# An LSTM with a low-rank adapter: VectorE transposes the pre-activations in PSUM instead of the hidden state in SBUF

## The reference

```python
def step(carry, xz_t):                      # LSTM: 16 sequences, 256 steps, 256 units
    prev_h, prev_c = carry
    z = xz_t + prev_h @ Wh                  # xz = x @ Wx + b, [16, 1024]
    ai, af, ao, ag = jnp.split(z, 4, axis=1)
    next_c = sigmoid(af) * prev_c + sigmoid(ai) * tanh(ag)
    next_h = sigmoid(ao) * jnp.tanh(next_c)
    return (next_h, next_c), next_h
x = x + lstm(x, cond)                       # [16, 256, 256]
# adapter: low-rank factors a1, b1, a2, b2 are made from cond by a small network
mid = gelu(x @ base_down + (x . a2) . b2)
out = mid @ base_up.T + (b1 . mid) . a1
x = x + out
```

## Time and profile before

| | us |
|---|---|
| median of 3 runs | 647.21 (644.83 to 648.85) |
| profiled execution, its time | 645.61 |
| profiled execution, its span | 643.6 |
| TensorE busy / VectorE / ScalarE | 604.5 / 430.3 / 412.8 |

### The profile page before, as it was taken

How to read it: one execution, slowest core, us unless ns; L and a number is a source line. 1 busy time by engine, 2 the same in 40 slices (tenths; PEclk the granted TensorE clock), 3 DMA queues, 4 the chain that set the end, 5 groups by cost and what they waited for, 6 DMA issues and landing times.

```text
span 643.6 us, 34068 instructions
## 1 busy us (share of the span) xinstructions
PE 604.5 (94%) x14176; PEld 450.4 (70%) x14176; DVE 430.3 (67%) x2292; ACT 412.8 (64%) x2414; POOL 38.2 (6%) x78
## 2 busy tenths in 40 slices
PE   8789999999998999999999999999999999999997
PEld 5555556777776677777777777777777777777876
DVE  3566556777776677677777777777777676777663
ACT  2465565666666666666666666666666666666672
POOL 3000000000000000000000000000000000000000
PEclk9799999999999999999999999999999999999999
DMA  4883522022223112322211222322123223212201
GB/s 160 223 210 130 175 43 42 22 29 52 53 52 53 28 33 48 53 52 53 52 33 29 47 53 52 53 52 38 26 45 52 53 52 53 39 35 25 54 20 34
DMA packets 31467, 38.71 MB, mean 60 GB/s; under 512 B 3601, under 2 KB 29505, under 8 KB 30290
## 3 DMA queue, kind: packets, MB, share of 16 engines
q1 hardware_dynamic: 31282, 36.51, 26.9%
q0 software_dynamic: 32, 0.03, 0.0%
HBM read 15.55 MB, written 4.19 MB: 31 GB/s over the span
## 4 chain that ended last, share of the span: by engine, by line
PE 63%; DVE 25%; ACT 6%; issue 4%; DMA 1%; SPq 0%; ACTq 0%; DVEq 0%
PE z L666 31%; PE x_bank L488 9%; DVE gates L815 8%; DVE prod L810 8%; PE aux L514 8%; ACT gates L405 6%; DVE h_t L825 5%; PE z_o L666 4%; PE out_bank L595 4%; DVE hid L820 3%; PE aux L499 2%; PE out_bank L545 1%; PE out_bank L537 1%; DMA seed<-proj 1%; PE x_bank L514 1%
## 5 line engine op out<-in xcount | busy, mean ns | idle before, releaser
L666 PE MATMUL z<-wh,h_t 128*16 128x96 f32 x8160 | 226.6, 249 | 26.7 <-DVE h_t L825 16.3
L666 PEld LDWEIGHTS z<-wh,h_t 128*16 128x16 f32 x8160 | 154.0, 96 | 132.3 <-DVE h_t L825 110.4
L810 DVE SCALAR_TENSOR_TENSOR prod<-gates 128x64 f32<-128x64 f32 x512 | 113.2, 221 | 155.5 <-ACT gates L405 140.7
L405 ACT ACTIVATE gates<-z 128x96 f32<-128x96 f32 x512 | 106.2, 250 | 149.9 <-PE z L666 149.5
L488 PE MATMUL x_bank<-wx,x_t 128*128 128x256 f32 x512 | 150.3, 398 | 0.5 <-ACT x_t L323 0.5
L415 ACT ACTIVATE tanc<-gates 128x32 f32<-128x32 f32 x512 | 114.5, 224 | 48.1 <-DVE gates L815 47.8
L329 ACT ACTIVATE z<-seed 128x96 f32<-128x96 f32 x512 | 125.1, 245 | 5.6 <-DMA seed<-proj 5.6
L825 DVE STREAM_TRANSPOSE h_t<-hid 128x32 f32<-128x32 f32 x512 | 108.4, 212 | 17.4
L815 DVE SCALAR_TENSOR_TENSOR gates<-prod 128x32 f32<-128x32 f32 x512 | 98.1, 192 | 17.5
L666 PE MATMUL z_o<-wh,h_t 128*16 128x64 f32 x4080 | 104.8, 219 | 1.6 <-issue 1.6
L820 DVE SCALAR_TENSOR_TENSOR hid<-gate_o,tanc 128x32 f32<-128x32 f32 x512 | 98.3, 192 | 1.2 <-ACT tanc L415 1.2
(11 more groups left out here) (106 smaller groups left out, 350.0 us busy)
## 6 DMA issues: line engine op xcount, KB each, us to landing
seed<-proj SPq DMA_DIRECT2D x128, 128.0 KB, 3.9
w<-in_L_cond_W SPq DMA_DIRECT2D x4, 2048.0 KB, 9.7
x_nat<-in_x SPq DMA_DIRECT2D x32, 128.0 KB, 3.8
out<-y_nat SPq DMA_DIRECT2D x32, 128.0 KB, 3.8
wx<-in_L_cond_Wx SPq DMA_DIRECT2D x2, 512.0 KB, 5.2
wh<-in_L_cond_Wh SPq DMA_DIRECT2D x2, 256.0 KB, 6.1
wh<-in_L_cond_Wh SPq DMA_DIRECT2D x1, 512.0 KB, 6.1
w<-in_L_cond_W SPq DMA_DIRECT2D x1, 256.0 KB, 4.3
```

Source lines behind the costliest of these rows:

```text
L405: act.activation(gates[s % 2][m][:, 0:GC], z_bank[m][:, 0:GC], ACT.Tanh, scale=0.25).then_inc(gates_ready[m], 1)
L666: ins = pe.matmul(dst, h_prev[:, kc, :], rhs, start=False, stop=(kc == 1), skip_group_check=True)
L810: dve.scalar_tensor_tensor(prod[m][:, :], now[:, 0:2 * C], 1.0, now[:, 2 * C:4 * C], ALU.add, ALU.mult).then_inc(prod_ready[m], 1)
```

## The change

VectorE transposes z within its PSUM bank as soon as it is complete: z_bank[m][:, 0:96] into columns 96 to 191 of the same bank (zt), and the 64 columns of o_bank into its columns 64 to 127 (zt_o). After that units are on partitions and the 16 batch rows are columns, so that the padding can be left out: the gates' tanh writes 48 columns instead of 96, the o gate's is one instruction of 32 columns instead of two, prod has 32 columns instead of 64, cell, tanc and hid have 16 instead of 32. The product that was hid goes straight into h_t, and the two transposes of hid are gone. tanc lies in PSUM: half 0 in a bank of its own, half 1 in o_bank behind zt_o. ScalarE's seed_o waits for h of half 1 (ht_ready[1]) besides, since it writes into the bank that holds tanc of half 1. The first of the new hidden products (new_hidden with m = 0) waits for the o gate and for tanc.

ScalarE's order is now: gates 0, gates 1, o gate, tanc 0, seed 0, tanc 1, seed 1, seed o. VectorE's is: turn 0, turn 1, prod 0, turn o, cell 0, prod 1, cell 1, hidden 0, hidden 1. TensorE's list is the same as before.

```diff
--- before.py
+++ after.py
@@ -108,11 +108,9 @@
 
         h_first = sb("h_first", [P, NM, B])
 
-        gates = [[sb(f"gates{i}_{m}", [P, GC + C]) for m in range(NM)] for i in range(2)]
-        gate_o = sb("gate_o", [P, OC])
-        prod = [sb(f"prod{m}", [P, 2 * C]) for m in range(NM)]
-        tanc = [sb(f"tanc{m}", [P, C]) for m in range(NM)]
-        hid = [sb(f"hid{m}", [P, C]) for m in range(NM)]
+        gates = [[sb(f"gates{i}_{m}", [P, 4 * B]) for m in range(NM)] for i in range(2)]
+        gate_o = sb("gate_o", [P, NM * B])
+        prod = [sb(f"prod{m}", [P, 2 * B]) for m in range(NM)]
         h_t = [sb(f"h_t{i}", [P, NM, TB, 32]) for i in range(2)]
 
         xp = [sb(f"xp{i}", [P, NM, P]) for i in range(2)]
@@ -129,6 +127,10 @@
         aux = psum("aux")
         out_bank = psum("out_bank")
         x_bank = [psum(f"x_bank{i}") for i in range(2)]
+        tanc_bank = psum("tanc")
+        tanc = [tanc_bank[:, 0:B], o_bank[:, 2 * OC:2 * OC + B]]
+        zt = [z_bank[m][:, GC:2 * GC] for m in range(NM)]
+        zt_o = o_bank[:, OC:2 * OC]
         mid_bank, up_bank = (aux, x_bank[0]), (out_bank, x_bank[1])
 
 
@@ -162,7 +164,8 @@
         prod_ready = [sem(f"prod_ready{m}") for m in both]
         cell_ready = [sem(f"cell_ready{m}") for m in both]
         tanc_ready = [sem(f"tanc_ready{m}") for m in both]
-        hid_ready = [sem(f"hid_ready{m}") for m in both]
+        turned = [sem(f"turned{m}") for m in both]
+        turned_o = sem("turned_o")
         ht_ready = [sem(f"ht_ready{m}") for m in both]
         xp_ready = sem("xp_ready")
         u_psum, u_ready = ([sem(f"{n}{i}") for i in lanes] for n in ("u_psum", "u_ready"))
@@ -401,26 +404,26 @@
                     ahead, s_next = (k, s + 1) if s < TB - 1 else (k.plus(1), 0)
 
                     def gates_of(m):
-                        act.wait_ge(z_ready[m], n)
-                        act.activation(gates[s % 2][m][:, 0:GC], z_bank[m][:, 0:GC], ACT.Tanh,
+                        act.wait_ge(turned[m], n)
+                        act.activation(gates[s % 2][m][:, 0:3 * B].rearrange("p (g b) -> p g b", b=B),
+                                       zt[m].rearrange("p (g c) -> p g c", c=C)[:, :, 0:B], ACT.Tanh,
                                        scale=0.25).then_inc(gates_ready[m], 1)
 
-                    def tanh_o(m):
-
-                        cols = slice(C * m, C * (m + 1))
-                        return act.activation(gate_o[:, cols], o_bank[:, cols], ACT.Tanh, scale=0.25)
+                    def tanh_o():
+                        act.wait_ge(turned_o, n)
+                        act.activation(gate_o[:, :].rearrange("p (m b) -> p m b", b=B),
+                                       zt_o.rearrange("p (m c) -> p m c", c=C)[:, :, 0:B], ACT.Tanh,
+                                       scale=0.25).then_inc(gate_o_ready, 1)
 
                     def tanh_cell(m):
                         act.wait_ge(cell_ready[m], n)
-                        act.activation(tanc[m][:, :], gates[(s + 1) % 2][m][:, GC:GC + C], ACT.Tanh,
+                        act.activation(tanc[m], gates[(s + 1) % 2][m][:, 3 * B:4 * B], ACT.Tanh,
                                        scale=0.5).then_inc(tanc_ready[m], 1)
 
                     gates_of(0)
                     gates_of(1)
-                    act.wait_ge(zo_ready, n)
-                    tanh_o(0)
+                    tanh_o()
                     tanh_cell(0)
-                    tanh_o(1).then_inc(gate_o_ready, 1)
                     if more:
                         act.wait_ge(gates_ready[0], n)
                         seed_bank(ahead.par, s_next, 0)
@@ -429,6 +432,7 @@
                         act.wait_ge(gates_ready[1], n)
                         seed_bank(ahead.par, s_next, 1)
                         act.wait_ge(gate_o_ready, n)
+                        act.wait_ge(ht_ready[1], n + 1)
                         seed_o(ahead.par, s_next)
 
                     if s == TB - 2 and (front or k.p == 0):
@@ -768,7 +772,7 @@
             dve.memset(zeros[:, :], 0.0).then_inc(zeroed, 1)
             dve.memset(hid_win[:, :, :], 0.0).then_inc(zeroed, 1)
             for m in both:
-                dve.memset(gates[0][m][:, GC:GC + C], 0.0).then_inc(zeroed, 1)
+                dve.memset(gates[0][m][:, 3 * B:4 * B], 0.0).then_inc(zeroed, 1)
 
             dve.wait_ge(b_psum, 1)
             dve.tensor_scalar(b_all[:, 0:2 * H], out_bank[:, :], 2.0, None, ALU.mult).then_inc(b_ready, 1)
@@ -803,26 +807,32 @@
             dve.wait_ge(consts_made, 2)
             dve.reduce_sum(own_row[:, :], ident[:, :].rearrange("p (r b) -> p b r", b=B), AX.X).then_inc(zeroed, 1)
 
+            def turn(m, n):
+                dve.wait_ge(z_ready[m], n)
+                dve.transpose(zt[m], z_bank[m][:, 0:GC]).then_inc(turned[m], 1)
+
+            def turn_o(n):
+                dve.wait_ge(zo_ready, n)
+                dve.transpose(zt_o, o_bank[:, 0:OC]).then_inc(turned_o, 1)
+
             def cell_products(s, m, n):
 
                 now = gates[s % 2][m]
                 dve.wait_ge(gates_ready[m], n)
-                dve.scalar_tensor_tensor(prod[m][:, :], now[:, 0:2 * C], 1.0, now[:, 2 * C:4 * C],
+                dve.scalar_tensor_tensor(prod[m][:, :], now[:, 0:2 * B], 1.0, now[:, 2 * B:4 * B],
                                          ALU.add, ALU.mult).then_inc(prod_ready[m], 1)
 
             def new_cell(s, m, n):
                 dve.wait_ge(prod_ready[m], n)
-                dve.scalar_tensor_tensor(gates[(s + 1) % 2][m][:, GC:GC + C], prod[m][:, C:2 * C], 0.5,
-                                         prod[m][:, 0:C], ALU.mult, ALU.add).then_inc(cell_ready[m], 1)
-
-            def new_hidden(s, m, n):
+                dve.scalar_tensor_tensor(gates[(s + 1) % 2][m][:, 3 * B:4 * B], prod[m][:, B:2 * B], 0.5,
+                                         prod[m][:, 0:B], ALU.mult, ALU.add).then_inc(cell_ready[m], 1)
+
+            def new_hidden(k, s, m, n):
+                if m == 0:
+                    dve.wait_ge(gate_o_ready, n)
                 dve.wait_ge(tanc_ready[m], n)
-                dve.scalar_tensor_tensor(hid[m][:, :], gate_o[:, C * m:C * (m + 1)], 1.0, tanc[m][:, :],
-                                         ALU.add, ALU.mult).then_inc(hid_ready[m], 1)
-
-            def transpose_hidden(k, s, m, n):
-                dve.wait_ge(hid_ready[m], n)
-                dve.transpose(h_t[k.par][:, m, s, :], hid[m][:, :]).then_inc(ht_ready[m], 1)
+                dve.scalar_tensor_tensor(h_t[k.par][:, m, s, 0:B], gate_o[:, B * m:B * (m + 1)], 1.0, tanc[m],
+                                         ALU.add, ALU.mult).then_inc(ht_ready[m], 1)
 
             def make_weights(k, s):
 
@@ -848,16 +858,17 @@
                     n = k.k * TB + (s + 1)
                     if s == 0 and k.at_least(2):
                         dve.wait_ge(xp_ready, k.k * 2 - 2)
+                    turn(0, n)
+                    turn(1, n)
                     cell_products(s, 0, n)
+                    turn_o(n)
                     new_cell(s, 0, n)
                     cell_products(s, 1, n)
                     new_cell(s, 1, n)
-                    new_hidden(s, 0, n)
-                    transpose_hidden(k, s, 0, n)
+                    new_hidden(k, s, 0, n)
                     if s == 7 and not front and k.p == 1:
                         mask_u(last_early)
-                    new_hidden(s, 1, n)
-                    transpose_hidden(k, s, 1, n)
+                    new_hidden(k, s, 1, n)
 
                     if s == 0 and a:
                         mask_u(a)
```

## The result

| | kernel before | changed kernel |
|---|---|---|
| median of 20 runs, us | 646.68 (644.83 to 649.39) | 649.68 (647.59 to 651.02) |
| profiled execution, span | 643.6 | 647.8 |
| VectorE / ScalarE busy | 430.3 / 412.8 | 453.2 / 373.7 |

The ratio is 1.0043, 95% interval [1.0031, 1.0056]: 2.8 us slower (the two medians differ by 3.0), where 6.6 were forecast. ScalarE does 9% less, VectorE 5% more. Neither figure tells what happened.

A forecast was written before the change was run, and what follows sets the result against it. It took h of half 1 to set the 2.32 us step, and seed 1 after the change, at 2.35; 221 steps x 0.03 = 6.6 us on the 647.2 median gave 653.8, so 654, range 641 to 671.

The forecast's parts named there:

- (0, 0): TensorE's first pair of a step, half 0 of h into z_bank[0]; forecast to start 1.52 us after turn 0.
- 9th load: TensorE's first weight load of its second pair, (0, 1), which waits for seed 1; forecast at 1.75 us.
- What bounds the kernel before: Path of a 2.32 us step through gates, VectorE and ScalarE to h of half 1; half 0 had 0.03 us to spare.
- TensorE's own need in the two heavy steps: TensorE's work with the filler in two of a block's eight steps, claimed to need 2.32 us whatever the chain.
- the rival of dear turns: PSUM makes VectorE's turns longer, turn 0 up to 342 ns: 669 or 685 us; chance 0.22 (662 to 685).
- The hidden state of half 1 comes 0.12 us earlier and isn't used: Hidden 1 ends at 1.72 instead of 1.84 us; TensorE would allow a 2.20 us step but waits for seed 1.
- seed 1 is what I think decides: ScalarE's seed 1, behind tanc 1, ends at 1.70 and delays TensorE's (0, 1) to 1.75: step 2.35 us.
- hidden 0 0.06 us below it: Path through VectorE's hidden 0, ending 1.465, TensorE at 1.52, (1, 0) at 1.86: step 2.29 us.
- The mark that I named for the seed: A hole of about 0.06 us between TensorE's 8th and 9th loads, ended by ScalarE, would show seed 1 decides.
- the 0.43 from (1, 0) to the next step: Time from TensorE's start of (1, 0), half 1 of h into z_bank[0], to the next step: 0.43 us.
- the two ranges that I had kept apart: Half 0 or near it, 641 to 649 us, chance 0.20; the forecast with the seed, 650 to 658, chance 0.50.
- The rival "the seed is in time and half 0 decides": Seed path falls under hidden 0's: step 2.29, heavy steps 2.32, -5 us, 642 us; chance 0.20.

The follow-up runs named there:

- experiments 3: Changed kernel with seeds 0 and 1 moved right behind the gates and the two waits of hidden 0 swapped: 633.50 us, ratio 0.9769 to the kernel before.
- experiment 7: Changed kernel with TensorE's order (0, 0), (1, 0), (0, 1), (1, 1), half 1 of h entering z_bank[0] second: 627.14 us, ratio 0.9699.
- 10: Changed kernel with early seeds, swapped waits and new TensorE order, plus filler pieces moved from steps 2 and 3 to 5 and 6: 631.51 us, ratio 0.9768.
- experiment 6: Changed kernel with tanc in SBUF again, 16 columns, nothing else changed: 654.63 us, ratio 1.0119 to the kernel before.
- experiment 2: Changed kernel with the two waits of hidden 0 written in the other order, tanc's last: 650.00 us, ratio 1.0022 to the kernel before.
- experiment 1: Changed kernel with ScalarE's seeds 0 and 1 moved from behind tanc 0 and tanc 1 to right behind the gates: 646.25 us, ratio 0.998.

## Why the prediction was off

On a clock from turn 0, forecast against the rows of the changed kernel (start less 337.63):

| | forecast | measured |
|---|---|---|
| gates 0 | 0.30 | 0.33 |
| turn o | 0.65 | 0.68 |
| cell 0 | 0.81 | 0.85 |
| tanc 0 | 1.02 | 1.06 |
| cell 1 ends | 1.31 | 1.29 |
| tanc 1 | 1.345 | 1.34 |
| seed 1 ends | 1.70 | 1.69 |
| hidden 0 ends | 1.465 | 1.52 |
| hidden 1 ends | 1.72 | 1.72 |
| (0, 0) | 1.52 | 1.57 |
| 9th load | 1.75 | 1.74 |
| step | 2.35 | 2.34 |

- What bounds the kernel before: right for h of half 1. TensorE's own need in the two heavy steps was put at 2.32; it is 2.307 (experiments 3 and 7, and 10 shows that it is TensorE's), so in before these too followed h of half 1, at 2.32.
- The turns: 277 ns in the mean for 96 columns against 270, 257 for 64 against 241. The one on the path, turn 0, took 298, 28 over the forecast and just over the 0.29 us from which I had said that the rival of dear turns begins to count. It came nowhere near that rival's 342. The row out of PSUM without a penalty was the right guide, and the Trainium skill's 65 ns for a PSUM source ("VectorE: DVE Perf Modes", section "The TRN2 errata") doesn't show: the hidden product reads tanc from PSUM in 171 ns, and from SBUF, in experiment 6, in 175.
- The hidden state of half 1 comes 0.12 us earlier and isn't used: right, and shown by experiment 7, where it is.
- **The step that failed is the one on which path decides: "seed 1 is what I think decides", with hidden 0 0.06 us below it.** Seed 1's path was sized right, 2.342 where it stands alone (experiment 2) against 2.35. Hidden 0's was mis-sized: 2.338 (experiment 1) against 2.29, and it is the one that sets the changed kernel's step, with seed 1 just in time. Its 0.05 us: turn 0 took 0.30 in the first position, not 0.27, and turn o 16 ns more, of which cell 0 gave half back by taking 154 ns and not 177; and tanc 0, which I let start as soon as cell 0 was there, waited behind the o gate, whose input is turn o, and which holds ScalarE for 93 ns. That wait is 0.03. Hidden 0 so ends 0.06 late, and the stretch from (1, 0) on is 0.01 shorter than forecast (see the size, below). Cell 0 ends at 338.48 + 0.15 = 338.63, tanc 0 starts at 338.69. Seed 1's path was spared, since cell 1 made up the loss.
- The mark that I named for the seed, a hole between the 8th and 9th load, was there and proved nothing, since the loads run a group ahead of the matmuls.
- The size: the step grew by 0.018 and not by 0.03. The term of the sum that was too large is the 0.43 from (1, 0) to the next step, which was 0.416. Some 10 ns of that are the new start after a wait, which in the row of before came from the wait for h of half 1, and which I counted again for a stretch that isn't interrupted there; the rest is rounding. 221 x 0.018 = 4.0 us. That isn't yet the 2.8 measured. In the two profiled executions, whose spans differ by 4.2, the single long steps take 1.3 us back (2.9 in before, 1.6 in the changed kernel), and the stretch ahead of the first step adds 1.1. How much of either is in the medians of 20 isn't known, so the last 1.2 us stay open.
- The sign was right in part by luck. The path that set the step was the one that I had priced as a gain, and 649.68 lies between the two ranges that I had kept apart, 641 to 649 for half 0 and 650 to 658 for the seed.
- The rival "the seed is in time and half 0 decides", to which I gave 0.20, had the mechanism right. With hidden 0 at its true size it gives 2.338, a loss of 0.018 and no gain.

## What to carry to other kernels

Where a step is closed by several waits of one engine, price each of the paths to it with the same care, queue positions on the other engines included, and expect a tie: removing one of two tied waits shows nothing, and only both edits together tell. A shorter chain for one operand pays when the consumer's order asks for that operand first; here the same change was 0.4% slower with the old order, 3% faster with the new one, and 2.3 to 3.2% faster with the old order and the longer queue positions cleared. Give a hole in the weight loads no weight before the matmuls behind it have moved too.

## What the hardware showed that I had not expected

- The second wait of a VectorE instruction cost 0.07 us when the wait written last was the one that ended last, and nothing in the other order: 0.102 from tanc 0's end to hidden 0's start in one order, 0.032 in the other (experiment 2).
- The same form has different durations by what stands ahead of it. Turn 0, after idle time, takes 298 ns, turn 1 right behind it 256, and 298 too in experiment 7, where it comes after idle time; cell 0 takes 154 ns behind turn o and 175 ns where prod stands ahead of it. The evacuation of x_bank, unchanged, went from 384 to 417 ns (before, then changed):

```profile
L743 DVE TENSOR_TENSOR proj<-x_bank,b_all 128x256 f32<-128x256 f32 x128 | 49.1, 384 | 5.1 <-PE x_bank L488 5.1
L747 DVE TENSOR_TENSOR proj<-x_bank,b_all 128x256 f32<-128x256 f32 x128 | 53.4, 417 | 6.2 <-PE x_bank L492 5.9 <-issue 0.3
```

- ScalarE's tanh of 16 columns from SBUF took 206 ns into SBUF (experiment 6) and 177 to 183 into PSUM (the changed kernel). The Trainium skill says the same of the direction ("ScalarE: Activation LUTs", section "Step-by-step: what each stage is for": PSUM is the lower-latency destination) without a number; here it is some 25 ns.
